# Another order of the attention stage: scale chain first, query last, row transposes in another bank

## The chip, the cores and the metric

One core of a Trainium2 chip runs the whole kernel. Its engines work side by side, each through its own list of instructions in a fixed order, and wait for one another by semaphores: TensorE (PE in the profile) multiplies and transposes, VectorE (DVE) and ScalarE (ACT) do element-wise work, GpSimd (POOL) issues here the gathers and scatters by index, SyncE (SP) issues plain transfers. The metric is the time of one execution in microseconds (us) on the device.

## The reference

The input is 8 sequences of 512 rows of 128 numbers. Three blocks follow one another, each adding to x:

```python
x = x + 0.5 * ffn(layernorm(x))      # experts: 8, two per row, at most 1024 rows each
x = x + attn(layernorm(x))
x = x + 0.5 * ffn(layernorm(x))
# attn: linear attention, 16 heads of 8
q = elu(h @ Wq.T + bq) + 1;  k = elu(h @ Wk.T + bk) + 1;  v = h @ Wv.T + bv
kv = einsum('bthd,bthe->bhde', k, v)
num = einsum('bthd,bhde->bthe', q, kv);  denom = einsum('bthd,bhd->bth', q, k.sum(axis=1))
out = (num / clip(denom, 1e-6)) @ Wo.T + bo
# ffn: softmax over 8 logits, the best two, a row's place in its expert by a running count,
#      relu(rows @ w1 + b1) @ w2 + b2, weighted sum of the two answers
```

## The kernel before

The kernel runs in stages: routing of the first expert block, its experts, then **the attention stage**, which the change touches, then the experts of the second block with their sums at the end. The attention stage does four things at once: it gathers the first block's answers and adds them (GpSimd gathers, `add_rows` on VectorE), normalises, does the attention, and routes the rows for the second expert block.

It walks through 8 groups, one sequence each, in 8 loop steps (s = 0 to 7) and a tail written out by hand. Every engine has its own list, in the functions `tensor`, `scalar` and `vector` of `Attention`. In step s:

- VectorE adds the gathered answers of group s (`add_rows`), takes statistics (`an_statistics`) and works out scale and shift for the layernorm in `scale_steps`: a chain of 13 small dependent pieces, the last of which releases `an_scale`. Of group s-2 it does the denominators and the division (`den_max`, `den_inverse`, `divide`). `den_max` stands behind the first piece of the scale chain and ahead of the second. Of group s-1 it does `q_sum`, `k_sum` and `kv_mask`; of group s-2, later in the step, `residual` and `statistics`. In steps 4 to 7 it also works through the second block's routing for pairs of groups (`row_scalar_steps` in 4 and 6, `top2_steps`, `gap_steps`, `place_steps` and `mark_steps` in 5 and 7).
- ScalarE does q's and k's exponentials of group s-1, copies v, copies the turned attention rows of s-2 (`attT_out`), applies the layernorm of group s (`norm`, waits for `an_scale`) and copies its transposes (`anT_out`). Of the routing it copies the finished rows' transposes (`turned_out`) and the logits (`raw_out`), and in steps 5 and 7 it writes normalised rows and the gates (`scalar_norm`, `scalar_gate`).
- TensorE turns the normalised group s (`turn`), multiplies it into q, keys and values (`q`, `kv`), sums keys times values of s-1 (`keysum`), multiplies q of s-1 with that (`query`), turns and projects the answers of s-2 (`turn_out`, `project`), and for the routing turns finished rows of s-3 (`self.route.turn`), takes logits of s-4 (`row_logits`) and counts (`counts`, steps 5 and 7). `fill` are matmuls whose result nobody reads. A copy of a transpose or product lives in one PSUM bank until another engine has read it; which bank that is sets which waits stand in the lists.
- GpSimd gathers 8 pieces per group, and then sends rows to their experts (`send`, line 839). The groups' rows go out in four parts of two groups, 16 sends each. Part 0 may go when step 5's marks are written, part 1 when step 7's are, parts 2 and 3 after marks in the tail. The second experts' stage starts reading when parts 0 to 2 have landed, and for its late blocks waits for part 3.

Lines of the kernel before that the text names: 1321 `turn`, 1328 `q`, 1337 `kv`, 1349 `keysum`, 1357 `query`, 1365 `turn_out`, 1373 and 1377 `project`, 490 and 502 the routing's turn and logits, 1312 `fill`; 1431 `norm`, 1439 `anT_out`, 449 `turned_out`, 454 `raw_out`, 1461 the copy of v; 1520 to 1547 the scale chain, 1556 `k_sum`, 1562 `q_sum`, 1569 `kv_mask`, 1574 `den_max`, 1585 `divide`, 1591 `residual`, 773 the first step of `place_steps` behind the counts, 822 the last of `mark_steps`.

Of the kernel before, what the change touches and what calls it, by code (L numbers as in the profile page):

```python
# [35 lines left out]
NG = NT // GT  # L36
# [70 lines left out]
def macaron(nc, x_in, Wq, bq, Wk, bk, Wv, bv, Wo, bo, wg, w1, b1, w2, b2, out):  # L107
    ctx = ExitStack()
    with ctx:
# [246 lines left out]
        def centred_out(act):  # L356

            act.wait_ge(WT_ps, 2)
            nc.scalar.copy(WT[:, 0:3].rearrange("p w c -> p (w c)"), bank[7][:, 0:3 * C]).then_inc(WT_sb, 1)

        def logit_bank(g):

            return bank[2] if g < NG // 2 else bank[6]
# [6 lines left out]
        class Route:  # L370
# [72 lines left out]
            def turned_out(self, act, g):  # L443

                f = self.f
                act.wait_ge(turned, NG * f + g + 1)
                if g >= 2:
                    act.wait_ge(logits_done, NG * f + g - 1)
                nc.scalar.copy(self.xT[:, g % 2], (turn_bank(g) if f == 0 else bank[0])[:]).then_inc(xnT_ready, 1)

            def raw_out(self, act, g):

# [23 lines left out]
            def turn(self, pe, g):  # L476

                f = self.f
                if f == 0:
                    pe.wait_ge(x_arrived[g % 4], 16 * (g // 4 + 1))  # L480
                    if g >= 2:
                        pe.wait_ge(xnT_ready, g - 1)
                else:
                    pe.wait_ge(x_summed, g + 1)
                    pe.wait_ge(anT_ready, min(g + 3, NG))
                    if g >= 1:
                        pe.wait_ge(xnT_ready, NG + g)
                to = turn_bank(g) if f == 0 else bank[0]
                for t in range(GT):
                    last = nc.tensor.transpose(to[:, t * P:(t + 1) * P], x_sb[:, GT * g + t], ident[:])  # L490
                last.then_inc(turned, 1)
# [794 lines left out]
        class Attention:  # L1286
# [21 lines left out]
            def tensor(self, pe):  # L1308
# [5 lines left out]
                def turn(n):  # L1314
                    pe.wait_ge(an_ready, n + 1)
                    if n >= 1:
                        pe.wait_ge(anT_ready, n)
                    if n >= 3:
                        pe.wait_ge(xnT_ready, NG + n - 2)
                    for t in range(GT):  # L1320
                        last = nc.tensor.transpose(bank[0][:, t * P:(t + 1) * P], self.an[:, n % 2, t], ident[:])
                    last.then_inc(an_turned, 1)
# [37 lines left out]
                def turn_out(n):  # L1360
                    pe.wait_ge(att_ready, n + 1)
                    if n >= 1:
                        pe.wait_ge(attT_ready, n)
                    for t in range(GT):
                        last = nc.tensor.transpose(bank[6][:, t * P:(t + 1) * P], self.att[:, n % 2, t], ident[:])
                    last.then_inc(att_turned, 1)
# [14 lines left out]
                for s in range(NG):  # L1381
                    if s >= 1:
                        fill(0, 4)
                    if s >= 3:
                        self.route.turn(pe, s - 3)
                    if s >= 2:
                        turn_out(s - 2)
                    if s >= 4:
                        self.route.row_logits(pe, s - 4)
                    if s >= 1:  # L1390
                        keysum(s - 1)
                    if s >= 2:
                        project(s - 2)
                    turn(s)
                    if s >= 1:
                        pe.wait_ge(qT_ready, s)
                        fill(1, 2)
                        query(s - 1)
                        fill(1, 4)
                    if s in (5, 7):  # L1400
                        self.route.counts(pe, (s - 5) // 2)
                    if s < NG - 1:
                        q(s)
                        kv(s)
                    else:
                        kv(s)
                        q(s)

                self.route.turn(pe, NG - 3)
                turn_out(NG - 2)  # L1410
# [14 lines left out]
            def scalar(self, act):  # L1425
# [43 lines left out]
                for s in range(NG + 1):  # L1469
                    if 1 <= s < NG:  # L1470
                        q_act(s - 1)
                        k_act(s - 1)
                    if s == NG:
                        k_act(NG - 1)
                        q_act(NG - 1)
                    if s >= 4:
                        self.route.raw_out(act, s - 4)
                    if s >= 2:
                        attT_out(s - 2)
                    if s < NG:  # L1480
                        norm(s)
                    if s >= 3:
                        self.route.turned_out(act, s - 3)
                    if s < NG:
                        anT_out(s)

                    if s in (5, 7):
                        self.route.scalar_norm(act, s - 5)
                        self.route.scalar_norm(act, s - 4)
# [15 lines left out]
            def vector(self, dve, ch):  # L1505
# [96 lines left out]
                for s in range(NG):  # L1602
# [5 lines left out]
                    if s >= 2:  # L1608
# [3 lines left out]
                        advance(scale, 1)  # L1612
                        divide(s - 2)
                        advance(scale, 1)
                    if s == NG - 1:
                        finish(scale)
                    if s >= 1:
                        q_sum(s - 1)
                        advance(scale, 3)
                        k_sum(s - 1)  # L1620
                    for _ in scale:
                        advance(others, 2)
                    if s >= 1:
                        kv_mask(s - 1)
                    finish(others)
# [13 lines left out]
                den_inverse(NG - 2)  # L1639
                divide(NG - 2)  # L1640
                advance(scalars, 6)
                k_sum(NG - 1)
                q_sum(NG - 1)
                kv_mask(NG - 1)
                advance(scalars, 6)
                den_max(NG - 1)
# [242 lines left out]
```

## Time and profile before

| | |
|---|---|
| median of 3 runs | 473.25 us (467.95 to 474.01) |
| the profiled execution's own time | 469.24 us |
| its span, first to last instruction | 467.5 us |
| granted TensorE clock, mean | 0.901 of full speed |
| busy: TensorE, VectorE, ScalarE, GpSimd | 77%, 75%, 51%, 60% of the span |

The profile is of one execution. Its time is 1.7 us above its span. Every timeline row gives the start in us from the span's start, how long the instructions of the row took, and in brackets how long the engine had been idle just before, with what ended the idle time. A busy share is an average over stages; what bounds a stage is read from the waits in it.

### The profile page before, as it was taken

How to read it: one execution, taken by the hardware profiler on the slowest of the kernel's cores; microseconds unless marked ns; L12 is line 12 of the kernel's file. 1: busy time of each engine (PE TensorE's matmuls, PEld its weight loads, DVE VectorE, ACT ScalarE, POOL GpSimd, SP SyncE). 2: the span in 40 equal slices, each digit the busy share in tenths (PEclk: the TensorE clock that was granted, in tenths of full speed). 3: DMA queues.
4: the chain of work that ended last, by engine and by line, in shares of the span. 5: the costliest groups of instructions: out<-in, count | busy, mean ns of one | idle time of the engine just before them, and what ended most of it. 6: DMA issues, size and time to landing. Idle time of an engine off the chain costs nothing.

```text
span 467.5 us, 6299 instructions
## 1 busy us (share of the span) xinstructions
PE 360.9 (77%) x1830; PEld 287.1 (61%) x1830; DVE 351.7 (75%) x1083; ACT 236.8 (51%) x431; POOL 278.6 (60%) x303
## 2 busy tenths in 40 slices
PE   7932879999999975889877978505799999999300
PEld 6912548888888733667665758405588888888200
DVE  6889178998888864688878885840489889889483
ACT  3688147667776604455354471420466776666100
POOL 9000577666664457777754636677767777776720
PEclk9999989999999989799889795756899999999855
DMA  8940314666666341121110101111622232311599
GB/s 229 356 159 1 96 46 133 208 201 194 222 225 219 117 131 51 52 57 51 53 45 25 53 25 52 52 57 58 202 69 77 82 93 90 92 46 41 163 326 296
DMA packets 47265, 55.50 MB, mean 119 GB/s; under 512 B 6694, under 2 KB 32832, under 8 KB 47232
## 3 DMA queue, kind: packets, MB, share of 16 engines
q1 hardware_dynamic: 34352, 35.40, 22.9%
q0 software_dynamic: 8512, 17.60, 12.9%
q10 hardware_dynamic: 4368, 2.10, 1.5%
q8 instruction: 15, 0.25, 0.2%
q14 instruction: 18, 0.15, 0.1%
HBM read 25.98 MB, written 29.10 MB: 118 GB/s over the span
## 4 chain that ended last, share of the span: by engine, by line
PE 54%; DVE 11%; DMA 7%; POOL 6%; ACT 6%; issue 4%; POOLq 0%; ACTq 0%; DVEq 0%; SPq 0%
PE psum L1056 6%; PE psum L1052 6%; PE psum L1069 6%; PE psum L1067 6%; PE psum L1068 6%; PE psum L1053 6%; PE psum L1078 3%; PE psum L1039 3%; POOL xg L1025 3%; PE psum L1357 2%; PE psum L1312 2%; DMA xs_dram<-xns,place 2%; PE psum L1337 2%; DMA xns<-yt_dram 2%; ACT an L1431 2%
## 5 line engine op out<-in xcount | busy, mean ns | idle before, releaser
L1121 ACT ACTIVATE hf<-psum,bcol 128x512 f32<-128x512 f32 x128 | 88.5, 691 | 64.8 <-PE psum L1056 61.6
L1025 POOL DMA_INDIRECT xg<-xn_dram,gidx x64 | 68.0, 1062 | 67.1 <-POOLq L1702 37.5
L1158 DVE TENSOR_TENSOR hl<-hf,hh 128x512 fp32r<-128x512 f32 x128 | 87.2, 691 | 5.1 <-ACT hh L1123 2.2
L1011 POOL DMA_INDIRECT yt_dram<-yg,target x64 | 74.2, 1159 | 27.7 <-issue 16.6
L839 POOL DMA_INDIRECT xs_dram<-xns,place x64 | 63.5, 992 | 40.0 <-DMA xs_dram<-xns,place 15.7
L1269 POOL DMA_INDIRECT yg<-y_dram,slot x64 | 61.2, 957 | 30.2 <-issue 19.3
L1052 PE MATMUL psum<-xh,wres 128*128 128x512 f32 x128 | 54.1, 422 | 3.4 <-ACT xh L1106 3.4
L1067 PE MATMUL psum<-hh,wres 128*128 128x512 f32 x128 | 53.0, 414 | 0.0
L1056 PE MATMUL psum<-xl,wres 128*128 128x512 f32 x128 | 51.4, 402 | 0.1
L1053 PE MATMUL psum<-xh,wres 128*128 128x512 f32 x128 | 50.9, 398 | 0.0
L1069 PE MATMUL psum<-hh,wres 128*128 128x512 f32 x128 | 50.5, 395 | 0.0
L1068 PE MATMUL psum<-hl,wres 128*128 128x512 f32 x128 | 50.2, 393 | 0.0
L1151 DVE CAST hh<-hf 128x512 fp32r<-128x512 f32 x96 | 44.3, 462 | 6.3 <-ACT hf L1121 5.8
L1147 DVE TENSOR_TENSOR xl<-psum,xh 128x512 fp32r<-128x512 f32 x32 | 21.9, 683 | 31.0 <-ACT xh L1106 31.0
L1106 ACT CAST xh<-psum 128x512 fp32r<-128x512 f32 x32 | 18.8, 587 | 30.7 <-PE psum L1039 28.8
L1312 PE MATMUL psum<-ones_bf 128*128 128x512 bf16 x94 | 27.9, 428 | 2.2 <-PEq L1796 2.2
L1052 PEld LDWEIGHTS psum<-xh,wres 128*128 128x128 f32 x128 | 24.5, 192 | 8.3 <-ACT xh L1106 4.4
L1056 PEld LDWEIGHTS psum<-xl,wres 128*128 128x128 f32 x128 | 24.5, 192 | 7.2 <-DVE xl L1147 1.8
L1069 PEld LDWEIGHTS psum<-hh,wres 128*128 128x128 f32 x128 | 24.2, 189 | 5.5
L1053 PEld LDWEIGHTS psum<-xh,wres 128*128 128x128 f32 x128 | 24.7, 193 | 4.2
L1068 PEld LDWEIGHTS psum<-hl,wres 128*128 128x128 f32 x128 | 24.3, 190 | 4.2
L1067 PEld LDWEIGHTS psum<-hh,wres 128*128 128x128 f32 x128 | 24.3, 190 | 3.7
(247 smaller groups left out, 726.3 us busy)
## 6 DMA issues: line engine op xcount, KB each, us to landing
yt_dram<-zeros SPq DMA_DIRECT2D x24, 256.0 KB, 3.5
xns<-yt_dram SPq DMA_DIRECT2D x24, 256.0 KB, 5.0
xs_dram<-zeros SPq DMA_DIRECT2D x16, 288.0 KB, 2.7
xg<-xs_dram SPq DMA_DIRECT2D x16, 288.0 KB, 2.8
wexp_raw<-in_L_ffn_w SPq DMA_DIRECT2D x16, 256.0 KB, 6.2
y_dram<-y_rows_out SPq DMA_DIRECT2D x16, 256.0 KB, 2.4
x_sb<-in_L_attn_x SPq DMA_DIRECT2D x8, 256.0 KB, 4.1
xn_dram<-xns SPq DMA_DIRECT2D x8, 256.0 KB, 5.9
```

What stands on the lines that cost most here:

```text
L839: gp.indirect_dma_start(out=xs_dram, out_offset=bass.IndirectOffsetOnAxis(ap=self.place[:, k, t:t + 1], axis=0), in_=self.xns[:, t // GT, ...
L1011: gp.indirect_dma_start(out=yt_dram, out_offset=bass.IndirectOffsetOnAxis(ap=target[:, j:j + 1], axis=0), in_=self.y_sb[:, s % YG, t], in_ ...
L1025: gp.indirect_dma_start(out=self.xg[:, s % 4, t], out_offset=None, in_=xn_dram, in_offset=bass.IndirectOffsetOnAxis(ap=gidx[:, j:j + 1], a ...
L1052: nc.tensor.matmul(bank[1 + c][:], w[:, 0, at], self.xh[:, s % 2], start=True, stop=False)
L1053: nc.tensor.matmul(bank[1 + c][:], w[:, 2, at], self.xh[:, s % 2], start=False, stop=False)
L1056: nc.tensor.matmul(bank[1 + c][:], w[:, 0, at], self.xl[:, s % 2], start=False, stop=True).then_inc(h_ready[c], 1)
L1067: nc.tensor.matmul(sums[:], w[:, 1, at], self.hh[:, s % 2, c], start=(c == 0), stop=False)
L1068: nc.tensor.matmul(sums[:], w[:, 1, at], self.hl[:, s % 2, c], start=False, stop=False)
L1069: last = nc.tensor.matmul(sums[:], w[:, 3, at], self.hh[:, s % 2, c], start=False, stop=(c == HC - 1))
L1121: one = nc.scalar.activation(self.hf[:, c], bank[1 + c][:], ACT.Relu, bias=bcol[:, at:at + 1])
L1158: dve.tensor_tensor(self.hl[:, s % 2, c], self.hf[:, c], self.hh[:, s % 2, c].bitcast(F32), ALU.subtract).then_inc(hl_ready[c], 1)
L1269: gp.indirect_dma_start(out=self.yg[:, n % YB, k, t], out_offset=None, in_=y_dram, in_offset=bass.IndirectOffsetOnAxis(ap=slot[:, k, GT * ...
```

## The change

The order of the three hand-written lists is changed; no product, sum or copy is added or removed except one `fill(1, 4)` per step.

VectorE: the rest of the scale chain of group s runs right behind `divide(s - 2)`, ahead of `q_sum` and `k_sum` of s-1. The routing's small steps of steps 4 and 6 are woven in one by one, and five of them stand between `k_sum` and `kv_mask`. TensorE: `turn(s)` now stands behind `keysum` and `row_logits` and ahead of `project` and the routing's turn; `q` and `kv` stand ahead of `query`. ScalarE: `raw_out` and `turned_out` change places around `norm` and `anT_out`. The routing's transposes go to bank 6 for groups 0 to 4, and their waits change with that.

```diff
+        def rows_bank(g):
+
+            return bank[6] if g < NG - 3 else bank[0]
+
@@ Route.turned_out, Route.turn
-                nc.scalar.copy(self.xT[:, g % 2], (turn_bank(g) if f == 0 else bank[0])[:]).then_inc(xnT_ready, 1)
+                nc.scalar.copy(self.xT[:, g % 2], (turn_bank(g) if f == 0 else rows_bank(g))[:]).then_inc(xnT_ready, 1)
-                    pe.wait_ge(anT_ready, min(g + 3, NG))
+                    if g >= NG - 3:
+                        pe.wait_ge(anT_ready, NG)
-                to = turn_bank(g) if f == 0 else bank[0]
+                to = turn_bank(g) if f == 0 else rows_bank(g)
@@ Attention.tensor: turn, turn_out
-                    if n >= 3:
-                        pe.wait_ge(xnT_ready, NG + n - 2)
+                    if n >= 2:
+                        pe.wait_ge(xnT_ready, NG + min(n - 1, NG - 3))
@@ the loop of TensorE
+                    if s >= 2:
+                        turn_out(s - 2)
+                    if s >= 1:
+                        keysum(s - 1)
+                    if s >= 4:
+                        self.route.row_logits(pe, s - 4)
+                    turn(s)
+                    if s >= 2:
+                        project(s - 2)
                     if s >= 3:
                         self.route.turn(pe, s - 3)
-                    if s >= 2:
-                        turn_out(s - 2)
-                    if s >= 4:
-                        self.route.row_logits(pe, s - 4)
-                    if s >= 1:
-                        keysum(s - 1)
-                    if s >= 2:
-                        project(s - 2)
-                    turn(s)
                     if s >= 1:
                         pe.wait_ge(qT_ready, s)
                         fill(1, 2)
+                    q(s)
+                    kv(s)
+                    if s >= 1:
                         query(s - 1)
-                        fill(1, 4)
                     if s in (5, 7):
                         self.route.counts(pe, (s - 5) // 2)
-                    if s < NG - 1:
-                        q(s)
-                        kv(s)
-                    else:
-                        kv(s)
-                        q(s)
@@ the loop of ScalarE
-                    if s >= 4:
+                    if s == NG:
                         self.route.raw_out(act, s - 4)
                     if s >= 2:
                         attT_out(s - 2)
                     if s < NG:
                         norm(s)
+                        if s >= 4:
+                            self.route.raw_out(act, s - 4)
+                        anT_out(s)
                     if s >= 3:
                         self.route.turned_out(act, s - 3)
-                    if s < NG:
-                        anT_out(s)
@@ the loop of VectorE, behind divide(s - 2)
-                    if s == NG - 1:
-                        finish(scale)
+                    for _ in scale:
+                        if s in (4, 6):
+                            advance(others, 1)
                     if s >= 1:
                         q_sum(s - 1)
-                        advance(scale, 3)
                         k_sum(s - 1)
-                    for _ in scale:
-                        advance(others, 2)
+                    if s in (4, 6):
+                        advance(others, 5)
                     if s >= 1:
                         kv_mask(s - 1)
@@ the tail of VectorE (ScalarE's step 8 likewise)
+                q_sum(NG - 1)
                 k_sum(NG - 1)
-                q_sum(NG - 1)
```

TensorE in step 4, before: logits, `keysum`, `project`, `turn`, two fills, `query`, four fills, `q`, `kv`.

```order
L502 MATMUL psum<-wgc,xT 128x8 x4
L1349 MATMUL psum<-vv,kk 128x129 x4
L1373 MATMUL psum<-bpair,ones 128x512
L1377 MATMUL psum<-WT,attT 128x128 x4
L1321 MATMUL psum<-ident,an 128x128 x4
L1312 MATMUL psum<-ones_bf 128x512 x2
L1357 MATMUL psum<-kv,qT 128x144 x4
L1312 MATMUL psum<-ones_bf 128x512 x4
L1328 MATMUL psum<-anT,WT 128x512
L1337 MATMUL psum<-WT,anT 128x256 x4
```

The same step now: `keysum`, logits, `turn`, `project`, the routing's turn, two fills, `q`, `kv`, `query`.

```order
L1352 MATMUL psum<-vv,kk 128x129 x4
L507 MATMUL psum<-wgc,xT 128x8 x4
L1324 MATMUL psum<-ident,an 128x128 x4
L1378 MATMUL psum<-bpair,ones 128x512
L1382 MATMUL psum<-WT,attT 128x128 x4
L495 MATMUL psum<-ident,x_sb 128x128 x4
L1317 MATMUL psum<-ones_bf 128x512 x2
L1331 MATMUL psum<-anT,WT 128x512
L1340 MATMUL psum<-WT,anT 128x256 x4
L1360 MATMUL psum<-kv,qT 128x144 x4
```

`query` was the third piece from `turn`; it is now the last of the step, behind `project`, the routing's turn, `q` and `kv`.

VectorE in step 3, before, from `q_sum` to `kv_mask` (`nwa` and `rsa` are the scale chain's tiles).

```order
L1562 SCALAR_TENSOR_TENSOR qT<-psum,qe 128x512
L1538 TENSOR_TENSOR nwa<-nwa 128x4
L1543 SCALAR_TENSOR_TENSOR nwa<-nwa 128x4
L1534 SCALAR_TENSOR_TENSOR nwa<-nwa 128x4
L1556 SCALAR_TENSOR_TENSOR kk<-psum,ke 128x512
L1538 TENSOR_TENSOR nwa<-nwa 128x4
L1543 SCALAR_TENSOR_TENSOR nwa<-nwa 128x4
L1534 SCALAR_TENSOR_TENSOR nwa<-nwa 128x4
L1538 TENSOR_TENSOR nwa<-nwa 128x4
L1543 SCALAR_TENSOR_TENSOR rsa<-nwa 128x4
L1547 SCALAR_TENSOR_TENSOR rsa<-agg,rsa 128x4
L1569 TENSOR_TENSOR kv<-psum,block_mask 128x128
```

And now, of the same step, from the fifth piece of the chain on.

```order
L1539 TENSOR_TENSOR nwa<-nwa 128x4
L1544 SCALAR_TENSOR_TENSOR nwa<-nwa 128x4
L1535 SCALAR_TENSOR_TENSOR nwa<-nwa 128x4
L1539 TENSOR_TENSOR nwa<-nwa 128x4
L1544 SCALAR_TENSOR_TENSOR nwa<-nwa 128x4
L1535 SCALAR_TENSOR_TENSOR nwa<-nwa 128x4
L1539 TENSOR_TENSOR nwa<-nwa 128x4
L1544 SCALAR_TENSOR_TENSOR rsa<-nwa 128x4
L1548 SCALAR_TENSOR_TENSOR rsa<-agg,rsa 128x4
L1563 SCALAR_TENSOR_TENSOR qT<-psum,qe 128x512
L1557 SCALAR_TENSOR_TENSOR kk<-psum,ke 128x512
L1570 TENSOR_TENSOR kv<-psum,block_mask 128x128
```

All of the chain stands ahead of the two sums, and nothing stands any more between `k_sum` and `kv_mask`.

## Rows read from the trace of the kernel before

**Rows 1.** The chain of waits: start us, us, what; the last send's landing, and the experts' first matmuls.
```profile
323.51 2.94 DMA xs_dram<-xns,place
...
329.17 0.67 PE psum L1039 x4
```

**Rows 2.** The timeline of GpSimd: the sends that begin parts 0, 1 and 2.
```profile
250.12 1.01 POOL L839 DMA_INDIRECT xs_dram<-xns,place  x1 [7.85 <-DVE xns L822]
...
279.93 0.97 POOL L839 DMA_INDIRECT xs_dram<-xns,place  x1 [7.20 <-DVE xns L822]
...
302.56 0.98 POOL L839 DMA_INDIRECT xs_dram<-xns,place  x1 [0.84 <-DMA xs_dram<-xns,place]
```

**Rows 3.** VectorE's waits, 194.85 to 279.1: who for whom, us in total, times, longest.
```profile
DVE kk L1556 <- ACT vv L1461: 5.1, 5, 1.1
DVE prod L773 <- PE psum L749: 2.3, 1, 2.3
DVE qT L1562 <- ACT qe L1449: 2.2, 3, 1.4
DVE kv L1569 <- PE psum L1349: 1.7, 3, 1.3
```

**Rows 4.** The timeline of VectorE in step 2.
```profile
194.85 0.19 DVE L1574 TENSOR_SCALAR den<-psum 128x64 f32<-128x64 f32 x1
...
200.88 0.16 DVE L1547 SCALAR_TENSOR_TENSOR rsa<-agg,rsa 128x4 f32<-128x4 f32 x1
```

**Rows 5.** The timeline of VectorE, step 5's end to step 7's.
```profile
246.87 0.53 DVE L773 SCALAR_TENSOR_TENSOR prod<-psum,pick 128x64 f32<-128x64 f32 x3 [2.30 <-PE psum L749]
...
251.44 0.19 DVE L1574 TENSOR_SCALAR den<-psum 128x64 f32<-128x64 f32 x1
...
263.40 0.19 DVE L1574 TENSOR_SCALAR den<-psum 128x64 f32<-128x64 f32 x1
...
266.58 0.16 DVE L1547 SCALAR_TENSOR_TENSOR rsa<-agg,rsa 128x4 f32<-128x4 f32 x1
268.24 0.69 DVE L1556 SCALAR_TENSOR_TENSOR kk<-psum,ke 128x512 f32<-128x512 f32 x1 [0.89 <-ACT vv L1461]
270.18 0.29 DVE L1569 TENSOR_TENSOR kv<-psum,block_mask 128x128 f32<-128x128 f32 x1 [1.25 <-PE psum L1349]
...
278.91 0.27 DVE L822 SCALAR_TENSOR_TENSOR xns<-share,gap 128x64 f32<-128x64 f32 x1
```

**Rows 6.** The timeline of TensorE in steps 3 and 4.
```profile
214.19 0.63 PE L1321 MATMUL psum<-ident,an 128*128 128x128 f32 x4 [0.61 <-ACT xT L449]
214.66 0.59 PE L1312 MATMUL psum<-ones_bf 128*128 128x512 bf16 x2
215.09 1.14 PE L1357 MATMUL psum<-kv,qT 128*128 128x144 f32 x8
216.07 1.03 PE L1312 MATMUL psum<-ones_bf 128*128 128x512 bf16 x4
216.93 1.02 PE L1328 MATMUL psum<-anT,WT 128*128 128x512 f32 x2
...
219.52 1.03 PE L1312 MATMUL psum<-ones_bf 128*128 128x512 bf16 x4
...
221.25 0.96 PE L502 MATMUL psum<-wgc,xT 128*128 128x8 f32 x8
...
223.37 0.50 PE L1373 MATMUL psum<-bpair,ones 2*128 2x512 f32 x1
...
227.15 0.63 PE L1321 MATMUL psum<-ident,an 128*128 128x128 f32 x4 [2.19 <-ACT xT L449]
```

**Rows 7.** Stretches: busy PE, PEld, DVE, ACT, POOL (instructions), PEclk, DMA share, GB/s.
```profile
225.00:227.00 2.00, 0.00 (x0) 0.00 (x0) 1.88 (x11) 2.00 (x5) 1.70 (x2) 1.00 0.24 66
228.20:231.50 3.30, 3.30 (x13) 2.36 (x12) 3.23 (x18) 0.21 (x1) 2.38 (x4) 0.50 0.17 50
255.60:262.20 6.60, 6.00 (x22) 4.64 (x22) 6.26 (x35) 2.72 (x6) 4.62 (x5) 0.50 0.16 54
```

More of the change, by code:

```diff
@@ L1473, in scalar @@
                     if s == NG:
+                        q_act(NG - 1)
                         k_act(NG - 1)
-                        q_act(NG - 1)
-                    if s >= 4:
+                    if s == NG:
                         self.route.raw_out(act, s - 4)
```

## The prediction

> **What bounds the kernel now.** I read the chain of waits first. The last part of it that the attention stage can move is the landing of a send, 2.94 us from 323.51; the second experts' stage reads what has landed and TensorE begins on it at 329.17 [rows 1]. From there to the end the work is that of the experts, which the change doesn't touch. Next the timeline of GpSimd: part 0 of the sends waited 7.85 us for VectorE's marks and part 1 waited 7.20 us; part 2 began at 302.56 behind a landing, not behind a mark [rows 2]. So from the marks of step 7 on (L822, ended at 279.18 [rows 5]) GpSimd is never out of work: **the start of the experts, and with it the end, moves by as much as the marks of step 7 move.** The marks of part 2 have room, since part 2 began 22.6 us after part 1 for GpSimd's own sends. The marks of step 7 are made by VectorE, so I asked what VectorE waited for from step 2 to those marks: 5.1 us in `k_sum` for the copy of v, 2.3 for the counts, 2.2 in `q_sum`, 1.7 in `kv_mask`, together 11.3 [rows 3]. No gain of the change can be more than about that.
>
> I write A for the moment when the scale chain of a step is done. It was 201.04 in step 2 [rows 4] and 266.74 in step 7 [rows 5]: 65.7 us for five steps.
>
> **What the change removes.** The wait for the copy of v stood in the middle of the scale chain, and the layernorm of the next group stood behind it: a round trip chain, `norm`, `turn`, `q` and `kv`, exponentials, `k_sum`, chain. Now the chain doesn't contain `k_sum`. How long it then takes the trace shows: in step 7 it already ran ahead of the sums, from `den_max` at 263.40 to 266.74, so 3.34 us [rows 5]. In step 2 it took 201.04 - 194.85 = 6.19 [rows 4]. That is a gain of 2.85 on that piece.
>
> **What it adds.** `den_max` of s-2 stands ahead of all but the first piece of the chain, and it needs the result of `query(s-2)`. That was the first real work behind `turn`; it is now the last of TensorE's step. The new round trip is: A, `k_sum`, `keysum`, (logits), `turn`, `project`, the routing's turn, fills, `q`, `kv`, `query`, `den_max`, chain, A. Its length from rows at the full clock:
> - A to the end of `keysum`: `q_sum` ahead of `k_sum`, taken as 0.6 (0.69 busy for the same shape, the next overlapping), and from the start of `k_sum` to `kv_mask`, which waits for `keysum`, 270.18 - 268.24 = 1.94 [rows 5]: 2.54. The layernorm lies beside that.
> - logits of step 4 on: 0.96. `turn`: 214.66 - 214.19 = 0.47. `project`: from 223.37 until TensorE fell idle at 227.15 - 2.19 = 224.96, so 1.59. The routing's turn is four transposes like `turn`: 0.47 from step 3 on. Two fills: 0.43. `q` and `kv`: 219.52 - 216.93 = 2.59. `query`: 0.98 [rows 6].
>
> The end of `query` is then at A + 8.60 in step 2, A + 9.07 in step 3, A + 10.03 from step 4 on. With 0.04 to hand over and 3.34 to the next A, a step takes 12.0, 12.4 and 13.4 us.
>
> VectorE alone would be at `den_max` earlier or about then. In step 4: `kv_mask` to A + 2.8, the rest of the routing's pieces 0.3, answers added by 4.2, `residual` not before `project` at 5.6, then 3.9 of sums and statistics: 9.5, against 10.1 by TensorE. The waits are near each other, so a shorter `query` path alone would give back 0.6.
>
> Step 5 is VectorE's. Its choices need the raw logits, which ScalarE now copies behind the layernorm: logits end at A + 3.5, copied 3.7. From the first choice to the end of the marks step 7 took 279.18 - 270.46 = 8.7 (the start 0.28 behind `kv_mask`), with no wait in it, and step 5 has 1.05 more for adding answers: marks at A + 13.5. From the first piece behind the counts to `den_max` it is 251.44 - 246.87 = 4.57 [rows 5], so `den_max` comes at A + 15.8. The next A comes 3.34 later, and 0.4 for the routing pieces woven in: 19.5. The wait of 2.30 for the counts goes, since they are done at about A + 10.4, before VectorE is there at 11.2. In step 7 they are just late: marks at A + 12.6, where it was 279.18 - 266.74 = 12.4.
>
> The beginning: `query(0)` used to be ahead of `q(1)` and `kv(1)`. Behind them `den_max(0)` is late by between nothing and 5.2 (2.59 at half clock). I take 1.7, since TensorE had some room before it: `den_max` at 196.6, A of step 2 at 200.0, a gain of 1.0.
>
> Sum: 200.0 + 12.0 + 12.4 + 13.4 + 19.5 + 13.4 = 270.7 for step 7, marks at 283.3. **That is 4.1 later than 279.18, at the full clock.**
>
> **The clock.** TensorE ran dry for 2.19 us before 227.15 [rows 6]. Soon after, the granted clock fell from 1.00 to 0.50 (1.2 instead of 2.4 GHz) and stayed there in 228.20 to 231.50 while TensorE was busy all of that time; another such stretch was 255.60 to 262.20 [rows 7]. The new order makes such a gap in every step. Behind `query` come four fills (0.86), then a wait for the division, `turn_out`, and a wait for `k_sum` of 2.5 us, because about 1.8 of the chain's 3.34 and 0.6 of `q_sum` and 0.7 of `k_sum` stand between the division and it. All that runs after the gap is on the round trip, so 3.3 us at half clock cost 1.65, and 6.6 us 3.3. I take 1.65 in five of the six steps from 2 to 7: the nearest row by size of the gap is the first, and one gap may pass without a fall. That is 8.3.
>
> The Trainium skill ("TensorE: Matmul & The Clock Gate", section "HAM oscillation — how this bites in real kernels") warns only of idle gaps longer than the one that I compute. By it the clock would stay high and the sum be 4.1 alone; the row of the 2.19 gap doesn't agree.
>
> **Edits at nothing.** The other bank for the routing's transposes takes the same four transposes and one copy; TensorE's waits on it are for copies of the step before. The turned-round `q_sum` and `k_sum` of the tail put `keysum(7)` up to 0.6 later; the cover is part 2's start, which waits for GpSimd's own sends [rows 2]. Without that cover it would be 0.6. The last four fills of a step that go away only fed the clock.
>
> **Sum.** 4.1 + 8.3 = 12.4 on the profiled execution's 469.24: **481.6**, taken as 481.5. That execution is 4 us below the median of the runs shown, 473.25, so against that median it is less than 2%.
>
> **Rivals.**
> 1. *The clock stays at 2.4 GHz.* For: a shorter gap, the 0.61 us ahead of 214.19 [rows 6], cost nothing. Against: the 2.19 us gap did. 469.24 + 4.1 = 473.3.
> 2. *Slow stretches of the longer kind.* Each gap is a little longer than 2.19 and has a second one beside it, as before 255.60. Five times 3.3 and 4.1: 489.8.
> 3. *Not slower: `query` is early enough.* If TensorE passes its pieces more tightly than my rows (`project` overlapping `anT_out`, the handovers of `keysum` shorter), so that `query` ends before VectorE is at `den_max`, then only VectorE's own order counts. It decides at A + 9.5 for `query` in step 4 and at about A + 8.3 in step 3. VectorE then waits 1.25 in `kv_mask` in steps 2, 3, 5 and 7, 0.2 in steps 4 and 6, and 0.9 for the raw logits in steps 5 and 7: 7.2 instead of 11.3. With 0.5 lost where the choices of step 5 are no longer woven with the chain: 3.6 faster, 465.6. For it: my lengths are near the limit. Against: the sum of TensorE's pieces on the trip has no wait in it that could shrink.
> 4. *Over 2% faster* would take 9.4 of the 11.3 us; nothing in the rows removes so much.
>
> **How the numbers follow.** The forecast, 476 to 487, has 0.48. Rival 1 has 0.19, rival 2 0.13, rival 3 0.15, rival 4 0.05. 2% is 9.4 us here, about what a measurement of this kernel can tell from no change: slower is above 478.6, faster below 459.8. Of the forecast 0.11 lies below 478.6. Slower: 0.37 + 0.13 = 0.50. Same: 0.11 + 0.19 + 0.15 = 0.45. Faster: 0.05. The range of 466 to 491 leaves out rival 4, half of rival 3 and the far end of rival 2. Its bounds also hold `den_max(0)` late by 0 to 5.2 instead of 1.7.
>
> **What the new profile would show.** Right, if VectorE's list of waits has `den_max` (the `den` tile) waiting for `query` in steps 2, 3, 4 and 6 and no longer `k_sum` for the copy of v; if `den_max` to A is 3.3 us everywhere; if `kv_mask` waits 1.25 in steps 2, 3, 5 and 7; if TensorE idles some 2.5 us ahead of `keysum` and the clock is 0.50 behind it in most steps; if part 1 of the sends begins some 12 us later than 279.93 and the experts with it. Wrong, if steps 3 and 4 take under 12 us, if the clock stays at 1.00 between 200 and 250, or if part 2 of the sends waits for marks, which would mean that the tail and not step 7 decides.

## The result and the profile after

The changed kernel takes **495.25 us** (median of 5 runs, 493.38 to 496.72), the kernel before 470.75 (5 runs). The ratio is **1.053**, 95% interval 1.049 to 1.056: 24.5 us slower. Ratios here and below leave out the runs that fell in a slower state, so they can differ from the ratio of the two medians. I forecast 481.5, range 466 to 491: the direction was right, the size was not, and the time lies outside the range. The profiled execution has a span of 494.9 us.

VectorE's waits from step 2 to the marks of step 7, as in [rows 3]:

```profile
DVE kv L1570 <- PE psum L1352: 11.3, 6, 2.2
DVE x_sb L1592 <- PE psum L1382: 10.2, 4, 3.5
DVE den L1575 <- PE psum L1360: 7.6, 5, 1.9
DVE prod L778 <- PE psum L754: 4.8, 2, 3.0
DVE first L591 <- ACT raw L458: 2.5, 2, 1.3
```

The 5.1 us for the copy of v are gone. All waits together are now 36.4 us, for TensorE (mask, `residual`, denominators, counts) and, through ScalarE, for the raw logits; before they were 11.3. VectorE in steps 2 and 3 (the last `rsa` row of a step ends at A), to be read against [rows 4]:

```profile
196.35 0.22 DVE L1575 TENSOR_SCALAR den<-psum 128x64 f32<-128x64 f32 x1 [1.88 <-PE psum L1360]
...
199.67 0.16 DVE L1548 SCALAR_TENSOR_TENSOR rsa<-agg,rsa 128x4 f32<-128x4 f32 x1
...
203.21 0.29 DVE L1570 TENSOR_TENSOR kv<-psum,block_mask 128x128 f32<-128x128 f32 x1 [2.18 <-PE psum L1352]
...
206.79 0.69 DVE L1592 TENSOR_TENSOR x_sb<-psum,x_sb 128x512 f32<-128x512 f32 x1 [2.16 <-PE psum L1382]
...
212.61 0.23 DVE L1575 TENSOR_SCALAR den<-psum 128x64 f32<-128x64 f32 x1 [1.86 <-PE psum L1360]
...
215.96 0.16 DVE L1548 SCALAR_TENSOR_TENSOR rsa<-agg,rsa 128x4 f32<-128x4 f32 x1
```

From `den_max` to A it is now 3.48 and 3.51 instead of 6.19, but the step from A to A is 216.12 - 199.83 = 16.3 us instead of 10.9. TensorE in the same step, against [rows 6]:

```profile
197.94 0.66 PE L1370 MATMUL psum<-ident,att 128*128 128x128 f32 x4 [0.77 <-DVE att L1586]
201.09 2.09 PE L1352 MATMUL psum<-vv,kk 128*128 128x129 f32 x8 [2.48 <-DVE kk L1557]
202.97 1.06 PE L1324 MATMUL psum<-ident,an 128*128 128x128 f32 x4
203.96 0.79 PE L1378 MATMUL psum<-bpair,ones 2*128 2x512 f32 x1
...
206.55 1.06 PE L1317 MATMUL psum<-ones_bf 128*128 128x512 bf16 x2
...
211.43 1.14 PE L1360 MATMUL psum<-kv,qT 128*128 128x144 f32 x8
```

There are two gaps, 0.77 and 2.48, and then everything runs at half speed: `project` takes 206.55 - 203.96 = 2.59 instead of 1.59. The gap ahead of `keysum` is 2.4 to 3.1 us in all six steps. The one ahead of `turn_out` is 0.77, but 5.30 in step 6. The stretches of the stage, with the granted clock as the third number from the end of each row (columns as in [rows 7]); first the kernel before from A of step 2 to the marks of step 7:

```profile
201.00:279.20 78.20, 67.14 (x374) 51.01 (x373) 65.21 (x311) 42.37 (x92) 46.82 (x49) 0.91 0.16 45
```

It has three slow stretches. Two are in [rows 7]; the third, in step 5, isn't:

```profile
241.90:245.20 3.30, 2.93 (x11) 2.53 (x12) 2.61 (x10) 2.03 (x6) 0.38 (x1) 0.50 0.07 24
```

The changed kernel, the same part of the program and then its slow stretches:

```profile
199.80:305.10 105.30, 80.65 (x356) 63.19 (x356) 67.48 (x313) 43.56 (x92) 47.08 (x50) 0.71 0.12 33
200.50:209.90 9.40, 8.81 (x27) 6.47 (x28) 4.99 (x19) 2.16 (x5) 6.83 (x8) 0.50 0.19 53
217.10:220.40 3.30, 3.02 (x13) 2.70 (x13) 1.12 (x6) 0.75 (x3) 2.69 (x3) 0.50 0.22 60
231.00:240.90 9.90, 9.10 (x36) 7.90 (x37) 4.90 (x22) 2.47 (x6) 4.71 (x5) 0.50 0.14 36
248.00:258.10 10.10, 8.90 (x36) 7.71 (x37) 6.22 (x24) 3.15 (x8) 0.00 (x0) 0.50 0.00 0
264.20:281.70 17.50, 10.85 (x41) 8.74 (x42) 12.36 (x65) 3.60 (x8) 11.76 (x12) 0.52 0.15 48
289.00:299.40 10.40, 9.64 (x37) 8.09 (x38) 6.53 (x25) 3.45 (x10) 0.00 (x0) 0.52 0.00 0
```

VectorE has about the same work in both (67.48 and 65.21 us), and the part is 27.1 us longer. There is a slow stretch in every one of the six steps. Only one has the 3.3 us that I took as the usual length, the others have 9.4 to 17.5. Last, GpSimd, against [rows 2]: part 1 of the sends and part 2.

```profile
305.85 0.97 POOL L844 DMA_INDIRECT xs_dram<-xns,place  x1 [18.54 <-DVE xns L827]
...
329.16 0.97 POOL L844 DMA_INDIRECT xs_dram<-xns,place  x1 [0.84 <-DMA xs_dram<-xns,place]
```

Part 1 starts 25.9 us later than before, and part 2 still waits for a landing and not for marks. So the tail hid what it was to hide, and the end moved with the marks of step 7, nearly: the span grew by 27.4.

### The profile page after: what moved, and what is told of

It reads as the page before. It is cut to its first block and busy times, and to the rows that moved or that the text cites. A ratio compares the mean times of both kernels' runs of the same rounds, so it can differ in the third digit from the quotient of the medians.

```text
span 494.9 us, 6242 instructions
## 1 busy us (share of the span) xinstructions
PE 374.3 (76%) x1802; PEld 299.6 (61%) x1802; DVE 355.6 (72%) x1083; ACT 237.5 (48%) x431; POOL 272.1 (55%) x303
## 5 line engine op out<-in xcount | busy, mean ns | idle before, releaser
L1163 DVE TENSOR_TENSOR hl<-hf,hh 128x512 fp32r<-128x512 f32 x128 | 88.3, 700 | 5.1 <-ACT hh L1128 2.0
L1016 POOL DMA_INDIRECT yt_dram<-yg,target x64 | 68.8, 1075 | 32.9 <-DVE yg L1181 16.6
L1057 PE MATMUL psum<-xh,wres 128*128 128x512 f32 x128 | 53.4, 417 | 3.4 <-ACT xh L1111 3.4
L1073 PE MATMUL psum<-hl,wres 128*128 128x512 f32 x128 | 50.3, 393 | 0.0
L1058 PE MATMUL psum<-xh,wres 128*128 128x512 f32 x128 | 50.1, 392 | 0.0
L1156 DVE CAST hh<-hf 128x512 fp32r<-128x512 f32 x96 | 45.6, 475 | 6.0 <-ACT hf L1126 5.7
L1352 PE MATMUL psum<-vv,kk 128*128 128x129 f32 x64 | 16.7, 442 | 22.2 <-DVE kk L1557 22.2
L507 PEld LDWEIGHTS psum<-wgc,xT 128*128 128x128 f32 x128 | 28.2, 324 | 3.1 <-ACT xT L453 2.9
L1057 PEld LDWEIGHTS psum<-xh,wres 128*128 128x128 f32 x128 | 24.2, 189 | 8.2 <-ACT xh L1111 4.4
L1352 PEld LDWEIGHTS psum<-vv,kk 128*128 128x128 f32 x64 | 14.3, 329 | 24.3 <-DVE kk L1557 24.2
L507 PE MATMUL psum<-wgc,xT 128*128 128x8 f32 x128 | 27.1, 341 | 2.4 <-ACT xT L453 2.4
L1074 PEld LDWEIGHTS psum<-hh,wres 128*128 128x128 f32 x128 | 24.2, 189 | 5.5
```

The source lines that it names most:

```text
L1016: gp.indirect_dma_start(out=yt_dram, out_offset=bass.IndirectOffsetOnAxis(ap=target[:, j:j + 1], axis=0), in_=self.y_sb[:, s % YG, t], in_ ...
L1057: nc.tensor.matmul(bank[1 + c][:], w[:, 0, at], self.xh[:, s % 2], start=True, stop=False)
L1058: nc.tensor.matmul(bank[1 + c][:], w[:, 2, at], self.xh[:, s % 2], start=False, stop=False)
L1073: nc.tensor.matmul(sums[:], w[:, 1, at], self.hl[:, s % 2, c], start=False, stop=False)
L1074: last = nc.tensor.matmul(sums[:], w[:, 3, at], self.hh[:, s % 2, c], start=False, stop=(c == HC - 1))
L1163: dve.tensor_tensor(self.hl[:, s % 2, c], self.hf[:, c], self.hh[:, s % 2, c].bitcast(F32), ALU.subtract).then_inc(hl_ready[c], 1)
```

## The experiments

Each ratio is to the kernel before on the same chip, with its 95% interval. The first question: is the loss the round trip, or the clock on it?

**1. Fills in the gaps of the changed kernel** (`e1_gap_fills`).

```diff
-                        fill(0, 4)
+                        fill(0, 24 if s == 6 else 7)
                     if s >= 2:
                         turn_out(s - 2)
                     if s >= 1:
+                        fill(0, {1: 20, 4: 13, 6: 13}.get(s, 10))
                         keysum(s - 1)
```

> Kernel: the changed one, with matmuls that nobody reads put where TensorE idled: 7 instead of 4 ahead of the turned answers (24 in step 6), 10 ahead of the key-value sum (20 in step 1, 13 in steps 4 and 6). Every dependency and every other order is that of the changed kernel. Theory (the round trip through the late query costs about 4 us, and TensorE at half clock along it the other 20): the clock stays at 1.00 through most of the stage, the steps fall to 12.0 to 13.4 us, and the time is 473 to 480, against 495 of the changed kernel. Rival (the loss is the waits that the new order makes, and the half clock only goes with them because TensorE idles): the granted clock rises, the steps stay at 16 to 18 us, the time stays above 490.

470.63 us, ratio 1.004 (1.000 to 1.009), below the 473 to 480 expected. Work that nobody reads, added to the list, gave back all of the loss of 5.3% but about 0.4 points. Its clock from A of step 2 to the marks:

```profile
198.30:280.60 82.30, 76.68 (x449) 52.71 (x447) 67.14 (x312) 43.52 (x92) 48.80 (x51) 1.00 0.16 44
```

And the ends of its scale chain in steps 2 to 5:

```profile
198.11 0.16 DVE L1549 SCALAR_TENSOR_TENSOR rsa<-agg,rsa 128x4 f32<-128x4 f32 x1
209.89 0.16 DVE L1549 SCALAR_TENSOR_TENSOR rsa<-agg,rsa 128x4 f32<-128x4 f32 x1
222.56 0.15 DVE L1549 SCALAR_TENSOR_TENSOR rsa<-agg,rsa 128x4 f32<-128x4 f32 x1
235.73 0.16 DVE L1549 SCALAR_TENSOR_TENSOR rsa<-agg,rsa 128x4 f32<-128x4 f32 x1
```

The steps take 11.8, 12.7 and 13.2 us, where the rows at full clock had given 12.0, 12.4 and 13.4. The next two take 19.3 and 13.2 (19.5 and 13.4 by the rows). From A of step 2 to the marks it is 82.3, against 83.3 by that sum and 78.1 before.

**2. Only the place of query undone** (`e2_query_first`).

```diff
                         fill(1, 2)
+                        query(s - 1)
                     q(s)
                     kv(s)
-                    if s >= 1:
-                        query(s - 1)
```

> Kernel: the changed one with one part undone: query of group s-1 stands again ahead of q and kv of group s. Theory (round trip plus half clock): the wait of the denominators for query goes (7.6 us in steps 1 to 7), the two pieces q and kv (2.6 at full clock) leave the round trip, but the gap ahead of the key-value sum stays and with it the half clock: 482 to 488. Rival (the place of query is the whole loss): 468 to 474. Second rival (keys and values now come late for the next step, so that another wait takes the place of the one removed): 492 or more, with the key sum waiting for the copy of v.

477.6 us, ratio 1.010 (0.998 to 1.022): better than the expected 482 to 488, and between the theories. The profile has 1.3 us of wait for `query` left instead of 7.6, no wait for the copy of v, and 8.7 us for `project`. The mean granted clock over 100 us from 199.9 is 0.82, where the changed kernel has 0.71 over its 105 us. The place of `query` is thus worth some 17 to 20 us (by the medians and by the ratios; the interval is wide) while the clock falls. There are three slow stretches between A of step 2 and the marks here and not six (212.80 to 216.10, 226.10 to 236.50, 257.20 to 270.60). How much of the gain is the shorter trip and how much the fewer stretches this run doesn't separate. It also shows that a gap need not bring the clock down: behind this one of 2.13 the clock stayed at 1.00 for the next 11.9 us (the second row is a stretch).

```profile
278.08 1.16 PE L1352 MATMUL psum<-vv,kk 128*128 128x129 f32 x8 [2.13 <-DVE kk L1556]
278.10:290.00 11.90, 9.06 (x64) 7.48 (x64) 9.21 (x41) 7.66 (x19) 0.20 (x1) 1.00 0.02 6
```

**3. VectorE's part of the change alone** (`e3_scale_only`), in the kernel before.

```diff
-                    if s == NG - 1:
-                        finish(scale)
+                    for _ in scale:
+                        if s in (4, 6):
+                            advance(others, 1)
                     if s >= 1:
                         q_sum(s - 1)
-                        advance(scale, 3)
                         k_sum(s - 1)
-                    for _ in scale:
-                        advance(others, 2)
+                    if s in (4, 6):
+                        advance(others, 5)
```

> Kernel: the one before with one part of the change alone: VectorE's list of the loop as in the changed kernel (scale chain ahead of the sums). Theory: this part by itself removes the waits for the copy of v (5.1 us) and brings a wait of 1.3 to 2.2 us in the mask of steps 2, 3, 5 and 7; TensorE idles ahead of the key-value sum, so the clock falls there in some steps: 468 to 476 against 470.75 of the kernel before. Rival (the moved scale chain is what makes the gap and so the slow clock): 485 or more. Rival (the chain ahead is a plain gain, and the rest of the change spoils it): under 466.

470.21 us, ratio 1.001 (0.996 to 1.006): no change. VectorE's waits from step 2 to the marks:

```profile
DVE kv L1569 <- PE psum L1349: 6.6, 6, 1.3
DVE x_sb L1591 <- PE psum L1377: 1.8, 2, 1.0
DVE kk L1556 <- ACT vv L1461: 1.7, 2, 1.0
```

One wait took the place of another, as expected. The gaps ahead of `keysum` in steps 2 to 4 are 1.3 to 1.5 us here, and the mean clock from 196.7 to 235 is 0.96, where the changed kernel fell to 0.50 in every step. It did fall once there, behind a gap of 1.29, and again from 247.20 to 260.60:

```profile
221.81 1.16 PE L1349 MATMUL psum<-vv,kk 128*128 128x129 f32 x8 [1.29 <-DVE kk L1556]
223.30:226.60 3.30, 3.30 (x15) 2.93 (x15) 2.49 (x11) 0.30 (x1) 2.38 (x4) 0.50 0.15 40
```

The kernel before has such stretches too, and the times are the same. So the moved chain alone does no harm.

**4. VectorE's part undone in the changed kernel** (`e4_scale_undone`): the reverse of the diff of experiment 3, and `raw_out` ahead of `attT_out` from step 4 on.

> Kernel: the changed one with VectorE's part of the loop undone (the scale chain again behind the key sum, as before), and the raw logits copied where they were before, since the choices wait for them. TensorE's new order stays. Theory: denominators still wait for the late query, and the chain behind them holds the two sums again, so the round trip is about as long, 12.9 us at full clock in step 3; the layernorm no longer waits behind the key-value sum. The half clock stays: 485 to 497. Rival (VectorE's order is what costs): 470 to 478.

500.42 us, ratio 1.064 (1.054 to 1.075), 3 us above the range expected. With the order of TensorE and the old chain the waits add up; in step 3:

```profile
214.01 0.66 PE L1370 MATMUL psum<-ident,att 128*128 128x128 f32 x4 [0.77 <-DVE att L1584]
215.82 1.16 PE L1352 MATMUL psum<-vv,kk 128*128 128x129 f32 x8 [1.16 <-DVE kk L1555]
218.56 0.66 PE L1324 MATMUL psum<-ident,an 128*128 128x128 f32 x4 [1.58 <-ACT an L1432]
```

The gap is split in two, 1.16 and 1.58, and the clock falls all the same, 2 us behind the start of the last row (0.76 on average in 219 to 222, and 0.71 over the 100 us from 200). **The order of TensorE does the harm without VectorE's new order, and VectorE's new order does none without TensorE's.** ScalarE's `norm` and `anT_out` stood ahead of `turned_out` here as in the changed kernel; no run undoes that alone.

**5. The bank of the rows' transposes undone** (`e5_rows_bank0`).

```diff
-            return bank[6] if g < NG - 3 else bank[0]
+            return bank[0]
...
-                    if g >= NG - 3:
-                        pe.wait_ge(anT_ready, NG)
+                    pe.wait_ge(anT_ready, min(g + 4, NG))
...
-                    if n >= 2:
-                        pe.wait_ge(xnT_ready, NG + min(n - 1, NG - 3))
...
+                    if s >= 4:
+                        pe.wait_ge(xnT_ready, NG + s - 3)
                     if s >= 1:
                         fill(0, 4)
```

> Kernel: the changed one with one part undone: the transposes of finished rows go to bank 0 again, with the waits that this needs (TensorE's routing turn behind the copy of the group's own transposes, the first fills of the next step behind the rows' copy). Theory: the copy of the group's transposes is long done when project ends, so no wait appears: 491 to 499, the same as the changed kernel. Rival (the bank matters, either way): 3 us or more off that.

491.73 us, ratio 1.048 (1.042 to 1.054), against 1.053 (1.049 to 1.056) of the changed kernel. The intervals overlap. TensorE's list of waits shows no new one. The bank costs nothing that these runs can tell.

**6. The fills that the change took away, given back** (`e6_fills_back`).

```diff
-                        fill(0, 4)
+                        fill(0, 8)
```

> Kernel: the changed one with the four fills per step given back that the change took away (8 instead of 4 behind query; they write bank 0, since bank 1 would be read meanwhile). They close most of the first, shorter gap of each step (0.77 us ahead of the turned answers), not the second (2.5 us ahead of the key-value sum). Theory (the second gap is what lowers the clock): little changes, 488 to 497. Rival (the fills that were taken away are the loss): 470 to 480.

495.68 us, ratio 1.052 (1.041 to 1.062). They were not the loss. They closed the first gap: TensorE waits once for the division, 4.4 us in step 6, and no longer six times, 9.1 in all. The clock fell as before, so the gap of 0.77 alone isn't what lowers it.

**7. The second gap filled alone** (`e10_second_gap`).

```diff
                     if s >= 1:
+                        fill(0, 10)
                         keysum(s - 1)
```

> Kernel: the changed one with 10 fills (2.1 us at full clock) in the second gap of each step alone, between the turned answers and the key-value sum. Closing the first gap alone changed nothing (495.7). Theory (the gap ahead of the key-value sum is what lowers the clock in steps 2 to 7; step 6 also has one of 5 us ahead of the turned answers, which stays): 472 to 480. Rival (both gaps are needed closed, since TensorE then still idles 0.8 us per step): above 485.

472.77 us, ratio 1.006 (1.001 to 1.012). The gap ahead of `keysum` is what lowers the clock in steps 2 to 5 and 7. The gaps ahead of `turn_out` stayed open, 13.4 us in seven places. Only in step 6, where that gap is 6.18, did the clock still fall, for 6.7 us:

```profile
252.30:259.00 6.70, 3.76 (x11) 1.91 (x12) 6.53 (x40) 1.88 (x5) 4.89 (x5) 0.50 0.13 44
```

Ten fills in another place of the step were not tried, so the runs don't say whether all ten have to stand in the gap.

**8. Half as many** (`e11_half_gap`): `fill(0, 5)` in the same place.

> Kernel: the same with half as many, 5 fills (1.1 us), so that 1.4 us of the second gap stay open. Theory (a gap of 1.3 us in the kernel before, ahead of 200.04, brought no fall, one of 2.2 us did): nearly as good as with 10, 473 to 482. Rival (half of the gap open is half of the loss): 483 to 490. Rival (it has to be closed): above 490.

482.04 us, ratio 1.018 (1.008 to 1.028). At the upper end of the theory's range. Its 4 runs spread from 475.3 to 485.7, much wider than those of `e10_second_gap` (471.7 to 474.1). The profiled execution is the slowest of the four, and it shows where the clock fell:

```profile
202.00:230.00 28.00, 21.88 (x130) 16.16 (x131) 22.73 (x106) 13.79 (x28) 21.12 (x22) 1.00 0.20 53
230.20:236.50 6.30, 6.30 (x20) 4.12 (x19) 3.79 (x15) 1.18 (x2) 4.83 (x5) 0.50 0.20 56
236.80:256.90 20.10, 14.87 (x93) 10.98 (x92) 14.84 (x68) 12.33 (x27) 5.41 (x6) 1.00 0.09 23
257.10:274.00 16.90, 13.52 (x46) 9.71 (x47) 11.73 (x63) 3.60 (x8) 11.79 (x12) 0.51 0.15 49
274.50:292.90 18.40, 14.42 (x93) 11.09 (x92) 13.08 (x61) 12.36 (x27) 3.87 (x4) 1.00 0.06 20
```

In steps 2, 3, 5 and 7 the gap that is left ahead of `keysum` is 1.3, and the clock stayed at 1.00. It fell in two of six steps: in step 4, where 2.04 was left open, and in step 6, where 6.18 stand ahead of `turn_out`. So half of the gap open isn't half of the harm in each step; most steps are free of it. This is one execution of four, and the faster ones have no trace.

The next question: does the kernel before lose to its clock too, and is there a version better than both?

**9. Fills in the kernel before** (`e8_before_fills`).

```diff
-                        fill(0, 4)
+                        fill(0, {1: 22, 6: 14}.get(s, 4))
...
+                    if s >= 1:
+                        pe.wait_ge(qT_ready, s)
+                        fill(1, {1: 6, 4: 9, 5: 11, 6: 2}.get(s, 0))
                     turn(s)
                     if s >= 1:
-                        pe.wait_ge(qT_ready, s)
...
+                fill(0, 12)
                 self.route.turn(pe, NG - 3)
```

> Kernel: the one before with fills in its own gaps (22 at the start of step 1, 14 in step 6, 6, 9, 11 and 2 ahead of the transposes of steps 1, 4, 5 and 6, 12 ahead of the tail). Its order is otherwise that of before. Theory (it too loses to the half clock, at four places of 3 to 10 us): 2 to 5 us faster, 464 to 468. Rival (its slow stretches lie beside VectorE's work, so nothing is gained): 469 to 473.

463.62 us, ratio **0.984** (0.974 to 0.994): so the kernel before does lose to its clock. From A of step 2 to the marks it is 74.0 us instead of 78.1, at full clock:

```profile
197.40:271.40 74.00, 69.21 (x411) 49.82 (x411) 65.15 (x311) 42.23 (x92) 47.99 (x51) 1.00 0.17 48
```

So at the same clock of 1.00 the two orders can be compared: 82.3 for the new one (experiment 1), 74.0 for the old one. The new order itself costs 8.3 us, twice what I had worked out, because I had compared it with an old order that was itself slowed. How much of the 8.3 is the round trip through TensorE is open: VectorE's part alone with fills (experiment 10) takes 77.0 in its profiled execution, with a slow stretch of about 3.4 us in it. By that, as an estimate, TensorE's and ScalarE's lists have 5 to 7 of the 8.3, and VectorE's the rest.

**10. VectorE's part with fills** (`e7_scale_fills`): experiment 3 with `fill(0, {1: 30, 5: 4, 6: 30, 7: 4}.get(s, 10))` at the start of the steps and `fill(0, 12)` ahead of the tail.

> Kernel: the one before with VectorE's part of the change and more fills at the start of the steps (10 in steps 2 to 4, 30 in steps 1 and 6, 12 ahead of the tail). The kernel with VectorE's part alone took 470.2. Theory (what is left there is the mask's wait for a key-value sum at half clock and the slow tail): the mask waits 1.3 instead of up to 2.2, 3 to 5 us gained, 463 to 468. Rival (the fills stand in the way of the turned answers or change nothing off the critical path): 469 to 473.

470.13 us, ratio 0.991 (0.985 to 0.997). Whether this is a gain is open: its 10 runs spread from 463.5 to 472.6, and the median of all of them is only 0.2% below the 471.27 of the kernel before on that chip. It is not better than the old order with fills.

**11. Work between the key sum and the mask** (`e9_rows_between`), on top of experiment 10.

```diff
                     if s in (4, 6):
                         advance(others, 5)
+                    elif 2 <= s < NG - 1:
+                        add_rows(dve, s + 1, 0)
...
-                    if s + 1 < NG:
+                    if s + 1 < NG and s not in (2, 3, 5):
                         add_rows(dve, s + 1, 0)
```

> Kernel: the same as the one before with VectorE's part of the change and more fills, and in steps 2, 3 and 5 the adding of the next group's first answers (1.1 us, four instructions) moved in between the key sum and the mask. Theory: the mask's wait of 1.3 in these steps is filled with work that stood behind it, 1.1 each: 3 us below the kernel with more fills alone, 460 to 465. Rival (the gathered answers are not there yet in steps 2 and 3, so VectorE waits for them instead): no gain over it, 463 to 468.

465.4 us, ratio 0.990 (0.979 to 1.000): no gain over experiment 10 that can be told. In step 3, at full clock, the mask waits 0.28 where it had waited 1.25, and what stood behind it waits in its turn, which it had not:

```profile
216.02 0.29 DVE L1570 TENSOR_TENSOR kv<-psum,block_mask 128x128 f32<-128x128 f32 x1 [0.28 <-PE psum L1349]
217.53 0.69 DVE L1592 TENSOR_TENSOR x_sb<-psum,x_sb 128x512 f32<-128x512 f32 x1 [1.14 <-PE psum L1377]
```

`residual` comes sooner and waits for `project`, as the kernel has it behind `keysum` on TensorE. Both theories had missed that. The two whole times don't price the move: this profiled execution also waited 2.70 us for a gather at 195.12, ahead of the moved work, and ran step 2 at half clock (200.60 to 207.20), which that of experiment 10 did not.

**12. The best of both** (`e12_hybrid`): experiment 9, and VectorE's new order in step 4 alone, where I expected it to shorten the step.

```diff
-                    if s == NG - 1:
-                        finish(scale)
+                    ahead = s in (4, NG - 1)
+                    if ahead:
+                        for _ in scale:
+                            if s == 4:
+                                advance(others, 1)
                     if s >= 1:
                         q_sum(s - 1)
-                        advance(scale, 3)
+                        if not ahead:
+                            advance(scale, 3)
                         k_sum(s - 1)
...
```

> Kernel: the one before with fills in its gaps (it took 463.6, 1.6% less than before), and VectorE's new order in step 4 alone, the step in which the chain ahead and the woven routing pieces shortened the step most; its fills stand at the start of that step. Theory: 1 to 1.5 us less than without that, 461 to 464. Rival (the step is bound elsewhere): 463 to 466.

461.69 us, ratio **0.984** (0.979 to 0.990): faster than before and than the changed kernel, not measurably faster than experiment 9. Nor is the little that it is ahead the work of VectorE's new order: its marks of step 7 end at 272.25, in experiment 9 at 271.46, and the experts' first matmul starts at 322.87 against 322.94.

## Why the prediction failed

*What bounds the kernel*: right. The marks of step 7 moved by 25.9 us, the experts' first matmul by 26.9, the span by 27.4, and part 2 of the sends waited for landings as before. Over all traces of this document the span is 186.1 to 191.1 us longer than the time of these marks, so the rule "the end moves by as much" is good to a few us.

*What is removed and added*: right in kind. The wait for v went, the chain took 3.5 instead of 6.2, and `den_max` waited for `query`. Its size at full clock was right to 1 us over five steps and the marks, as experiment 1 shows. The waits of `den_max` for `query` are in steps 2, 3, 4, 5 and 7; the list of signs had 2, 3, 4 and 6.

*The beginning*: A of step 2 was forecast at 200.0 and came at 199.83. That is luck: the 1.7 in it was picked between 0 and 5.2 for the full clock, and at full clock (experiment 1) A came at 198.27.

**The step that failed is the term for the clock**: "1.65 in five of the six steps", 8.3 us. That a gap in every step would bring the clock down was right; the length of the slow stretches was mis-sized, and the term measured 23.0. The clock fell in six of six, and the stretches were 9.4 to 17.5 us in five of them. The difference between the changed kernel and experiment 1, which is the same order with most of the gaps filled, is 24.6 us in the medians and 23.0 from A of step 2 to the marks (105.3 against 82.3). I had both lengths in the rows, 3.3 after the gap of 2.19 and 6.6 after the one with a second idle spell beside it [rows 7]. I took the first "by size of the gap", although the new gaps were longer than 2.19 and had a second one (0.77) beside them, so the second row was the nearer one. I wrote that down as the case against myself, under rival 2, and gave it 0.13. The third stretch of the kernel before, which I didn't read, was again 3.3, behind a gap of 2.68: size alone spoke for the short kind, and five of the six stretches were long. The gap of 5.30 in step 6, with the longest stretch behind it, wasn't in my sum at all. What the term comes to, seen afterwards, is half of the work in the slow stretches: TensorE was busy for 50.3 us of the six (8.81 + 3.02 + 9.10 + 8.90 + 10.85 + 9.64), and half of that, 25.2, is near the 23.0.

A second thing went unseen, though most of it is in the same rows. The old order too was slowed, in 228.20 to 231.50 and 255.60 to 262.20, and in 241.90 to 245.20. Without that it takes 74.0 and not 78.1 from A of step 2 to the marks (experiment 9). The term "4.1 later at full clock" compared a new order at full clock with an old one that wasn't, so the order's own price is 8.3.

*The rule weighed against the row*: by the Trainium skill ("TensorE: Matmul & The Clock Gate", section "HAM oscillation — how this bites in real kernels") the gap computed would have been harmless. It was not: in steps 2 to 5 and 7, whose longest gap is 2.4 to 3.1 us, the clock came down each time (in experiment 4 also behind 1.16 and 1.58 close together), as the row of 2.19 had said.

*The rivals*: rival 1 (full clock) is what experiment 1 made, and it came 2.7 us below its time, 470.6 where 473.3 was said; the 1.7 of the beginning is most of that. Rival 3 (not slower) fell with the 7.6 us of waits for `query`. Rival 2 had the right mechanism and still too short stretches.

What stays open: why a stretch lasts 3.3 us in step 3 and 9 to 10 in steps 2, 4, 5 and 7. In step 3 TensorE's gap was 2.51, as long as in steps 2, 5 and 7 (2.48, 2.38 and 2.38). In experiment 6 steps 2 and 3 both had the short kind, behind 2.41 and 2.38. Nor does the length of one gap tell whether the clock falls: behind 1.29 it fell once (experiment 3), behind 2.13 it once didn't (experiment 2).

## What to carry to other kernels

When a reorder leaves TensorE idle for 2 us or more in every turn of a loop whose round trip goes through it, price the half clock first and the order second: here they were 23.0 and 4.2 us of the same 27 us (8.3 for the order, against the old one at full clock). Compare two orders at the same clock, by filling the gaps of both, before judging either. And where a piece is moved ahead of another, ask who waits for the one that is now last: `query` stood right behind `turn`, and the next step's chain begins with its result.

## What the runs showed of the hardware

- Matmuls that nobody reads, 0.21 us each, put into idle time of TensorE gave 22 to 25 us back in one order (experiments 7 and 1) and 7.7 in the other (experiment 9). The granted clock from A of step 2 to the marks rose from 0.71 to 1.00 (experiment 1) and from 0.91 to 1.00.
- Four such matmuls per step behind `query` changed nothing (495.7 against 495.25), ten ahead of `keysum` gave nearly everything back (472.8), five in the same place more than half (482.0).
- The profiled execution of the changed kernel had TensorE busy 81 us between A of step 2 and the marks, 13.5 more than before with 18 matmul records fewer: busy time can rise because the engine is slow. Its share of the stretch fell, from 86% to 77%.
